# Edge maxima of the first four node pairs found tile by tile, and of the next four in one pass, in the stage of their sums

## What is computed

```python
# N = 6250 nodes, E = 106250 edges sorted by dst, D = 256, H = 4 heads of 64
ft = (layernorm(x) @ W).reshape(N, H, 64)
e_src, e_dst = sum(ft * w_att_src, -1), sum(ft * w_att_dst, -1)
e = e_src[src] + e_dst[dst];  e = where(e >= 0, e, 0.2 * e)
ex = exp(e - segment_max(e, dst)[dst])
a = ex / segment_sum(ex, dst)[dst] * dist
x = x + segment_sum(ft[src] * a, dst)
f = layernorm(x)
w = softmax(mean(f, 0) @ Wr + br)          # the outer axis has one entry, so w is one row of gates per node
h = relu(bn(f @ W1[e] + b1[e]));  h = relu(bn(h @ W2[e] + b2[e]))     # 8 experts, 256 wide
x = x + sum_e w[e] * (h @ Wo[e] + bo[e])
```

## Time and profile before

| | us |
|---|---|
| median of 3 runs | 1573.62 (1572.95 to 1577.39) |
| profiled execution | 1574.9, of it the span 1573.3 |
| TensorE busy in the span | 1473.4 (94%) |
| VectorE busy | 1186.0 (75%) |
| GpSimd busy | 1073.4 (68%) |
| ScalarE busy | 748.8 (48%) |

### The profile page before, as it was taken

How to read it: one execution, slowest core, us unless ns; L and a number is a source line. 1 busy time by engine, 2 the same in 40 slices (tenths; PEclk the granted TensorE clock), 3 DMA queues, 4 the chain that set the end, 5 groups by cost and what they waited for, 6 DMA issues and landing times.

```text
span 1573.3 us, 23952 instructions
## 1 busy us (share of the span) xinstructions
PE 1473.4 (94%) x8358; PEld 1294.1 (82%) x8358; DVE 1186.0 (75%) x2195; ACT 748.8 (48%) x1341; POOL 1073.4 (68%) x951
## 2 busy tenths in 40 slices
PE   6904799899999999999999999999999999999998
PEld 5703588788898888888888888888888888888887
DVE  7725446588888888888888888888888888888741
ACT  3600323345545554555555455555555555555553
POOL 4175576677787778778777777877887787787000
PEclk9956899999999999999999999999999999999999
DMA  8775345434434444443444344344434434443000
GB/s 228 209 231 177 103 117 136 109 99 137 115 104 132 123 123 108 134 115 104 130 122 128 100 138 116 104 131 122 125 102 138 116 103 131 120 124 87 11 6 9
DMA packets 106070, 187.50 MB, mean 119 GB/s; under 512 B 38357, under 2 KB 70490, under 8 KB 105919
## 3 DMA queue, kind: packets, MB, share of 16 engines
q0 software_dynamic: 44688, 123.13, 28.7%
q1 hardware_dynamic: 60701, 62.29, 13.5%
q10 hardware_dynamic: 560, 0.52, 0.1%
HBM read 172.72 MB, written 14.42 MB: 119 GB/s over the span
## 4 chain that ended last, share of the span: by engine, by line
PE 89%; DVE 3%; POOL 3%; DMA 2%; issue 1%; ACT 1%; SPq 0%; ACTq 0%; DVEq 0%; POOLq 0%
PE bankH L791 43%; PE bankY L820 21%; PE bankE L750 7%; PE bankE L751 6%; PE bankB L728 3%; PE bankE L743 3%; POOL gath L642 3%; PE bankA L768 1%; DMA table<-gath 1%; PE bankE L670 1%; DMA gath<-table,src_win 1%; DVE gath L1399 1%; PE bankA L760 1%; PE bankE L785 1%; PE bankB L670 1%
## 5 line engine op out<-in xcount | busy, mean ns | idle before, releaser
L642 POOL DMA_INDIRECT gath<-table,src_win x900 | 1052.9, 1170 | 335.7 <-issue 249.3
L997 ACT ACTIVATE h<-bankH,bn_shift,bn_scale 128x250 f32<-128x250 f32 x800 | 401.6, 553 | 462.2 <-PE bankH L791 462.1
L791 PE MATMUL bankH<-xT,w 128*128 128x250 f32 x1600 | 378.4, 379 | 1.8 <-ACT xT L983 1.4
L820 PE MATMUL bankY<-wo,h 128*125 128x256 f32 x1600 | 378.6, 379 | 1.1 <-DVE x L1474 1.1
L791 PE MATMUL bankH<-h,w 128*128 128x250 f32 x1600 | 379.1, 379 | 0.0
L820 PEld LDWEIGHTS bankY<-wo,h 128*125 128x125 f32 x1600 | 296.3, 188 | 43.3 <-issue 1.4
L791 PEld LDWEIGHTS bankH<-h,w 128*128 128x128 f32 x1600 | 299.5, 191 | 35.7
L791 PEld LDWEIGHTS bankH<-xT,w 128*128 128x128 f32 x1600 | 296.8, 192 | 34.0 <-ACT xT L983 1.1
L1405 DVE TENSOR_TENSOR msg_lo<-gath,msg_hi 128x2340 fp32r<-128x2340 f32 x88 | 228.5, 2597 | 94.0 <-ACT msg_hi L969 94.0
L969 ACT ACTIVATE msg_hi<-gath 128x2340 fp32r<-128x2340 f32 x88 | 189.1, 2149 | 193.7 <-PE bankE L751 193.7
L1474 DVE SCALAR_TENSOR_TENSOR x<-bankY,gate,x 125x256 f32<-125x256 f32 x400 | 174.1, 477 | 120.3 <-PE bankY L820 120.0
(11 more groups left out here) (189 smaller groups left out, 922.8 us busy)
## 6 DMA issues: line engine op xcount, KB each, us to landing
onehot_t<-dst_low SPq DMA_DIRECT2D x48, 576.0 KB, 5.3
gath<-table,src_win POOLq DMA_INDIRECT x900, 2.9
x_res<-in_x SPq DMA_DIRECT2D x25, 250.0 KB
out<-x SPq DMA_DIRECT2D x25, 250.0 KB
table<-gath SPq DMA_DIRECT2D x25, 227.5 KB
w<-in_L_ffn_W SPq DMA_DIRECT2D x8, 512.0 KB, 10.6
gath<-in_x SPq DMA_DIRECT2D x5, 672.0 KB
wo<-in_L_ffn_Wo SPq DMA_DIRECT2D x4, 512.0 KB, 10.7
```

The source lines that it names most:

```text
L642: pool.indirect_dma_start(gath[:, g.slot(u), t, :], None, table, bass.IndirectOffsetOnAxis(src_win[:, g.win, u, t:t + 1], 0)).then_inc(row ...
L791: mm = pe.matmul(target[:, hc * 2 * NT:(hc + 1) * 2 * NT], weights[:, e * KC + c, hc * P:(hc + 1) * P], operand(c), start=(c == 0), stop=( ...
L820: mm = pe.matmul(bankY[0:NT, u * D:(u + 1) * D], h2[:, e % 2, c, u, :], wo[:, e * KC + c, :], start=(c == 0), stop=(c == KC - 1))
L997: ins = act.activation(target[:, e % 2, hc, :, :].rearrange("p u n -> p (u n)"), source[:, hc * 2 * NT:(hc + 1) * 2 * NT], ACT.Relu, bias= ...
```

## The change

- The plan of each pair has a list `passes` of (step, tiles). Pairs 0 to 3 get two passes, one for each tile, both in the stage where the pair is g: at steps 0 and 3 (pairs 0 and 2), 1 and 4 (pair 1), 0 and 2 (pair 3). Pairs 4 to 7 get one late pass for both tiles, at step 1 (pair 4) or 0. Before, pairs 1 and 2 had one late pass, the others none. From pair 8 on everything is as before.
- Scans end a step (`begins`), joins and weights stand in the next (`ends`), messages where `products` says.
- In plans with `rush` (pairs 0 to 7) `add_y`, the second `residual`, `norm1` and `make_onehot` stand in this order and ahead of the scans of a; in `STEADY` the order is the old one.
- Which chunks are summed in two parts is told by `low`: pairs 0 and 1 none, pair 2 all but chunk 2, pair 3 all, pair 4 all but chunk 0, then all. Before: pairs 0 to 2 none.
- GpSimd's rows of pairs 0 to 8 wait by one list: none up to row 22, 40 rows in stage 0, 42 in stage 1, 40 each in stages 2 to 5.
- SyncE loads the window of a pair with two passes later, and behind the store of the result.

```diff
-SOON = ((2, (0,)), (3, (1,)), (4, (2,)), (5, (3,)))
-STEADY = Plan(0, dict(SOON), 1, 3, {3: (0,), 4: (1,), 5: (2,), 6: (3,)}, {5: (0,), 6: (1,)}, 7)
-PLANS = {0: Plan(0, dict(SOON), 1, 3, {3: (0,), 4: (1,), 5: (2,), 6: (3,)}, {5: (0,), 6: (1,)}, 6, low=False),
-         1: Plan(3, {5: (0,), 6: (1, 2, 3)}, 4, 5, {6: (0,), 7: (1, 2, 3)}, {7: (0, 1)}, 8, runs=2, low=False),
-         2: Plan(2, {4: (0, 1), 5: (2, 3)}, 3, 4, {5: (0, 1), 6: (2, 3)}, {5: (0,), 6: (1,)}, 7, runs=1, low=False)}
+    def __init__(self, sums, place=1, bounds=3, new=1, rows=3, onehots=None, residuals=None, turn=7, products=None,
+                 passes=((None, (0, 1)),), low=(), rush=True):
+        self.products = products or {s - 1: chunks for s, chunks in sums.items()}
+PLANS = {0: Plan({2: (0,), 3: (1,), 5: (2,), 6: (3,)}, place=2, new=5, rows=5, onehots={3: (0, 1), 7: (2, 3)},
+                 residuals={3: (0,), 6: (1,)}, passes=((0, (0,)), (3, (1,)))),
+         1: Plan({3: (0,), 4: (1,), 6: (2, 3)}, new=6, rows=6, onehots={4: (0, 1), 7: (2, 3)},
+                 residuals={4: (0,), 6: (1,)}, passes=((1, (0,)), (4, (1,)))),
+         2: Plan({3: (0,), 4: (1,), 5: (2,), 6: (3,)}, new=5, rows=5, onehots={6: (0, 1), 7: (2, 3)},
+                 residuals={5: (0,), 6: (1,)}, products={1: (0,), 2: (1,), 4: (2,), 5: (3,)}, passes=((0, (0,)), (3, (1,))), low=(0, 1, 3)),
...
+for n in (5, 6, 7):
+    PLANS[n] = Plan({3: (0,), 4: (1,), 5: (2,), 6: (3,)}, new=2, onehots={4: (0,), 5: (1,), 6: (2,), 7: (3,)},
+                    residuals={5: (0,), 6: (1,)}, passes=((0, (0, 1)),), low=ALL)
...
+            early = [None] * (TE + 5) + released((
+                (runs_turned, 1, 2), (carry_back, 1, 5), (msg_ready, 1, 1), (agg_done, 1, 2), (agg_done, 2, 6),
...
+                *(event for f in range(2, 6) for event in stage(f, full)), *stage(6, full[:FROM + 1])))
...
+                    for k, tiles in plan.begins(s):
+                        turn_runs(g, k)
                     if a is not None and not late(a) and s == 6:
-                        turn_runs(a)
+                        turn_runs(a, 0)
```

More of the change, by code:

```diff
@@ L88 @@
 class Plan:
[L91 to L100, removed]
@@ L114, in late, with lows, last_low, found @@
 def late(g):
-    return g is not None and plan_of(g).runs is not None
+    return g is not None and plan_of(g).passes[0][0] is not None
+def lows(g, c):
+    return sum(len(plan_of(Pair(n)).low) for n in range(g.n)) + sum(k < c for k in plan_of(g).low)
+def last_low(g, c):
+    for order in reversed(range(g.n * CHUNKS + c)):
+        if order % CHUNKS in plan_of(Pair(order // CHUNKS)).low:
+            return order + 1
+    return None
+def found(g, k):
+    return sum(len(plan_of(Pair(n)).passes) for n in range(g.n)) + k + 1
 def before(f, s, steps):
@@ L604, in _, with stage @@
-            early = {0: {}, 1: dict(enumerate(second)), 2: dict(enumerate(third)), 3: dict(enumerate(fourth))}
-            assert len(second) == len(third) == len(fourth) == 2 * TE
+            def stage(f, behind):
+                done = (f + 1) * CHUNKS
+                for step, rows in enumerate(behind):
+                    done += len(plan_of(Pair(f + 1)).sums.get(step, ()))
+                    for sem, count, r in zip((h1_done, h2_done, y_done, agg_done),
+                                             (f * EX + step + 1, f * EX + step, f * EX + step - 1, done), rows):
+                        if r:
+                            yield sem, count, r
@@ L852, in body @@
                             out_bias(f)
-                    if late(g) and s == plan.logits:
-                        turn_carry(g)
+                    for k, tiles in plan.ends(s):
+                        turn_carry(g, k)
                     if a is not None and s == plan.bounds:
@@ L1024, in body @@
                         relu1(f, s)
[L1025 to L1026 removed]
+                    if g is not None and not late(g) and s == 0:
+                        exp_logits(g, 0, (0, 1))
                     if run and s == 0:
@@ L1044, in body @@
                         keep_gate(f)
-                    if late(g) and s == plan.runs:
-                        keep_esrc(g)
-                    if late(g) and s == plan.logits:
-                        exp_logits(g)
-                    if g is not None and plan.low:
+                    for k, tiles in plan.begins(s):
+                        keep_esrc(g, k, tiles)
+                    for k, tiles in plan.ends(s):
+                        exp_logits(g, k, tiles)
+                    if g is not None:
                         for c in plan.sums.get(s + 1, ()):
-                            keep_high(g, c)
+                            if c in plan.low:
+                                keep_high(g, c)
             def path():
@@ L1534, in body @@
                                 residual(g, u)
-                    if a is not None and late(g) and s == plan.bounds + 2:
-                        row_bounds(a)
-                    if a is not None and late(g):
+                    if plan.rush:
+                        if run and (s >= 2 or not f.begins(1)):
+                            add_y(*before(f, s, 2))
                         for u in plan.residuals.get(s, ()):
```

191 lines of the change are left out of this document (94 added, 97 removed).

## The result

| | before | after |
|---|---|---|
| median of 4 runs, us | 1575.47 (1572.95 to 1577.39) | 1602.26 (1600.58 to 1605.45) |
| profiled execution, span | 1574.9, 1573.3 | 1601.73, 1600.0 |

The ratio is 1.0181, with a 95% interval of 1.0167 to 1.0194: slower by 1.8%, some 27 us, where I had forecast 13.4 and a range up to 1596. Lines of the kernel after are 41 higher on TensorE (L751 turns the scans, L757 the joins, L784, L791 and L792 sum, L832 and L861 are the layers); L1375 and L1376 are VectorE's scans, L993 ScalarE's copy.

What follows compares the result with a forecast made beforehand. TensorE bounds the kernel from stage 2 on. Start -7.4, stage 0 +1.2, stage 1 -12.0, stages 2 to 5 +6.1, +4.8, +6.2, stage 6 +12.2, clock +2.3: +13.4, 1587.0 us; forecast 1583 to 1591, range 1575 to 1596.

Steps and rivals of the forecast that it cites:

- 2.7 and 6.4: Stage 0: TensorE's waits before turning the scans of the first pass, 2.7 us, and of the second, 6.4 us.
- 1.8 and 3.9: Stage 2: TensorE waits 1.8 us for scans, 3.9 us for a second pass's scans behind add_y, a message and bias.
- 5.2 and 3.9: Stage 6: TensorE waits 5.2 us for pair 8's scans behind pair 7's last sum, 3.9 us for the joins.
- the price of the clock: Stage 6: half clock behind the 5.2 us wait costs 2.3 us; none counted behind waits of 3.9.
- the first rival: Stages 2 to 6: 3.9 us waits also drop the clock, VectorE's chain costs more; 1592 to 1596; 0.18 with another.
- GpSimd "doesn't add to the sum": GpSimd's 40 rows a stage take 59.3 us; stages of 58 to 61 us just hold them, so nothing is added.
- The start: Stage -1: with tile 0 in its own pass, stage 0 starts at 158.1, 7.4 us earlier.
- Case 2: Low parts on time: stages 3 to 6 lose 1.3 us less each, stage 1 1.7 less; 1580 us; chance 0.12.
- case 4: Stages 2 to 6: VectorE reaches scans before the turn, 1.7 us each plus 1.8 of native sums; 1566; chance 0.07.
- Case 3: GpSimd's rows hold pairs 4 to 8, five stages of 59.3 us; no change, about 1575 us; chance 0.08.
- stage 7 on at 55.1 again: Test on the trace after: from stage 7 on, stages take 55.1 us again, as before the change.
- the copy of stage 3 that a row releases: Test: GpSimd's rows releasing ScalarE's copies in stages 3 to 6 would show the forecast wrong.

Runs made afterwards that it cites:

- the first and the third experiment: Against the changed kernel: first, stage 6's scans and joins moved ahead on VectorE, 1588.17 us; third, unread matmuls in four TensorE waits, 1593.09 us.
- both edits: Changed kernel with stage 6's VectorE order swapped and, where late passes begin, scans moved ahead of add_y: 1580.22 us, ratio 1.003.

## Why the prediction was wrong

**Direction and mechanism held, the size didn't: 13.4 us of 27.** The waits, step by step:

- Stage 0: 2.22 and 6.06 for 2.7 and 6.4. Stage 1: 1.79 and a late low part of 1.59 for 1.7 and 1.7. Stage 2: 1.79 and 3.41 for 1.8 and 3.9. Stages 4 to 6: 1.72 and 1.35 (in stage 6 1.71) for 1.8 and 1.3. Stage 6: 5.15 and 3.80 for 5.2 and 3.9. The 6.4, 5.2 and both 3.9 came from counting VectorE's instructions ahead of the need, and that way of counting is right to half a microsecond. The small ones were carried over from the row of 1.72, and 2.7 was a guess between two rows. In stage 1 the number was luck: the wait was forecast for the second scans, which have none, and stands at the first.
- **The step that failed is the price of the clock.** I had put half clock behind waits of 5 us and more only, since 5.11 and 5.13 had shown it and 1.72 had not, and had left everything between to the first rival, with a chance of 0.18 together with another. It costs 4.5 us at the start of stage 7 (behind 3.80) and 3.0 in stage 2 (behind 3.41), as the run with the waits filled shows. The bound from both sides was there; in the middle of it I took the cheap end for the sum and the dear one for a rival. That rival's 1592 to 1596 was nearest to what came, and it, too, was short: it took 2.3 for each, what 5.13 had cost. At the start of stage 7 the clock stayed low for 9.4 us (605.6 to 615.0) instead of the 5 behind 5.13. Another wait of 5.15 had ended 12 us before, but that this is the reason isn't shown: with the order of stage 6 changed, the clock was low for 12 us behind the 3.41 of stage 2.
- **GpSimd "doesn't add to the sum" was wrong at one place.** In stage 3 the scans wait for a row of pair 4: 2.79 us instead of 1.8. I had weighed 40 rows against the length of a stage, but a pass needs its last row at a step, not at the stage's end. The weighing itself was off: a row of 2.90 is 1.95 longer than one of 0.95, not 2.3, which gives 57.8 us for 40 rows instead of 59.3.
- The start: stage 0 began 2.4 us later than forecast. The two sums behind the second pass took 11.18 us for 9.99 and started 1.6 late. Part of this is the spread between executions: in the first and the third experiment, which change nothing up to there, stage 0 starts at 157.4 and 160.6.
- Case 2 (low parts on time) and case 4 (scans hidden) fell: the low parts of stages 3 to 6 waited 1.35 to 1.71. Case 4's point of decision was the residual of pair 7 between its last sum and the scans of pair 8; moved out of there, stage 6 fell by 11.3 us, which is that mechanism shown by intervention. Case 3 did not come as a length of stages, with both edits stages 4 to 6 take 57.6 to 58.7 us; its sign, a row that releases ScalarE's copy, came in stage 3 alone.
- Of my tests for the changed kernel, three failed: "stage 7 on at 55.1 again" (59.7), stage 2 at 61 (64.4), and the copy of stage 3 that a row releases. The first two told where to look.

**Why the change loses.** Stage 2 starts 16.3 us earlier (292.4 for 308.8), and the change pays for that in six stages that had no wait of TensorE of half a microsecond: by the table, stages 2 to 7 are 9.3, 5.8, 3.6, 3.5, 15.9 and 4.5 us longer, 42.35 together by the starts of stage 8 (665.59 and 639.57). 42.35 - 16.33 = 26.0 of the 26.7 between the spans. 15.9 of this is the order of stage 6, with its echo in stage 7, and 4.6 the scans behind `add_y` in stage 2.

## What to carry to other kernels

An engine that is full to 100% has no place for a pass that another engine has to finish within it: each one put there costs the waits between the engines (in stages 4 and 5 1.72 for the scans and 1.35 for a low part, of 3.5 in all), while an early stretch that already waits can be shortened at most by what it waits. When a chain moves, write out the instructions of the other engine between the last release and the next need; here that count gave the large waits to half a microsecond. Then price the clock behind each of them by a range and not by one row: here it cost 1.8 to 4.5 us behind waits of 3.4 to 6.1, and least behind the longest. And look for cheap swaps of order (the two here were worth 22 of the 27 us) before judging the idea.

## What the runs showed of the hardware

- On the first chip TensorE's clock was at its lower level behind every wait of 3.41 to 6.06 us in stages 0 to 7, and at the full one behind every wait of up to 2.79. The length of the wait doesn't tell for how long: 3 us behind 3.96, 8 behind 4.08 (0.50 from 371.5 to 379.5), 12 behind a 3.41, with TensorE busy throughout.
- Nor is the length of the wait all that decides whether it falls. On the later chips the clock stayed full behind a wait of 3.92 (1.00 from 309.2 to 320.0), and fell behind one of 2.22 (0.52 from 172.3 to 175.3). The first is from stage 2 of the version with stage 0 filled (batch 4), the second from stage 0 of the one with the waits filled (batch 3):

```profile
309.21 0.28 PE L755 MATMUL bankC<-ident,prefix 128*8 128x128 f32 x1 [3.92 <-DVE suffix L1389]
...
309.43 1.86 PE L836 MATMUL bankH<-xT,w 128*128 128x250 f32 x8
```

```profile
172.03 0.28 PE L755 MATMUL bankC<-ident,prefix 128*8 128x128 f32 x1 [2.22 <-DVE suffix L1389]
...
172.26 3.38 PE L836 MATMUL bankH<-xT,w 128*128 128x250 f32 x8
```

- Matmuls that nobody reads, put in place of the wait, keep the clock (1.00 for 0.56) and made the kernel 9.2 us faster with 39 matmuls more.
- A row that GpSimd issues beside a low part of VectorE took 2.69 to 3.37 us in stage 2 of the profiles from the first chip, and 2.20 where it met only the rest of one, instead of 0.95.
- With 72 rows fetched without pacing VectorE stood for 69.5 us with no releaser that the profile can name, and the kernel was 10.6% above the kernel before.
- The kernel before takes 1574 us in the first runs and the first batch and 1648 to 1658 on the chips of the four later batches; with both edits TensorE is busy there for 292.0 of 300 us, not 299.8. The kernel with both edits was at 1.003 of the kernel before on the first (1.0017 to 1.0043) and at 1.0005 on a later one (0.9985 to 1.0026), so a difference of a few tenths of a per cent has to be measured on each.
